# Scoring rows turned on TensorE, and a difference step that makes its state first

## The reference

```python
r = sigmoid(i_r + h_r); z = sigmoid(i_z + h_z)       # i = x @ W_ih + b_ih, h = state @ W_hh + b_hh
n = tanh(i_n + r * h_n)
state = (1 - z) * n + z * state                      # 1024 steps, one after the other
...
xn = (x - mean) * rsqrt(var + 1e-5) * gamma + beta
input_sigs = sign(xn)                                # 1024 signs per token
tile_sigs[e, features of e] = sign(mean(slopes[e]))  # zero elsewhere
best cluster = argmax over 8 of input_sigs @ cluster_sigs.T
tile_idx     = argmax of input_sigs @ tile_sigs.T within that cluster
u = clip((x_slice - min of the expert) / (max - min + 1e-8)); out = (base + slope * local) * scale
```

## Time and profile before

| | |
|---|---|
| median of three runs | 2458.68 us |
| the profiled execution, its own time | 2458.56 us |
| its span, first to last instruction | 2457.0 us |
| TensorE busy | 2338.7 us, 95% |
| VectorE, ScalarE, GpSimd busy | 1298.6, 658.6 and 215.8 us |
| difference stage | 2151.3 to 2358.4 us, 207.1 us |
| tail | 2358.4 to 2457.0 us, 98.6 us |

### The profile page before, as it was taken

The page is one execution under the profiler, slowest core; times in us unless marked ns, Lnnn a source line. Parts: engine busy times, 40 slices in busy tenths (PEclk is TensorE's granted clock), DMA queues, the critical chain, the costliest instruction groups (busy, mean ns, idle before and its releaser), DMA issues.

```text
span 2457.0 us, 83441 instructions
## 1 busy us (share of the span) xinstructions
PE 2338.7 (95%) x35188; PEld 1285.9 (52%) x35188; DVE 1298.6 (53%) x2691; ACT 658.6 (27%) x1333; POOL 215.8 (9%) x440
## 2 busy tenths in 40 slices
PE   7999999999999999999999999999999999977736
PEld 3444444444444445555666666666666666643412
DVE  4322121212122357676666655666666667788877
ACT  3200000000001133333333332333333333355530
POOL 0000000000000000000000000111111111123225
PEclk9999999999999999999999999999999999999965
DMA  7693131313143455454444444444444444478830
GB/s 238 206 338 126 51 129 52 129 52 128 48 145 103 154 166 157 139 158 123 136 133 132 132 142 103 117 118 120 113 119 116 115 120 121 117 228 232 234 89 5
DMA packets 177346, 330.78 MB, mean 135 GB/s; under 512 B 24272, under 2 KB 87168, under 8 KB 176192
## 3 DMA queue, kind: packets, MB, share of 16 engines
q1 hardware_dynamic: 145360, 267.53, 34.8%
q0 software_dynamic: 7680, 17.57, 4.9%
q10 hardware_dynamic: 24192, 44.05, 4.8%
HBM read 222.39 MB, written 156.77 MB: 154 GB/s over the span
## 4 chain that ended last, share of the span: by engine, by line
PE 51%; DVE 5%; DMA 3%; issue 2%; POOL 1%; ACT 0%; DVEq 0%; SPq 0%; POOLq 0%; ACTq 0%
PE banks L605 45%; PE banks L653 2%; DMA hs_scratch<-h 2%; PE banks L654 2%; PE banks L655 2%; DMA x_keep<-hs_scratch 1%; POOL y L1581 1%; DVE banks L1562 0%; DVE n_sum L912 0%; DVE sums L917 0%; PE banks L1487 0%; DVE z_old L902 0%; DVE rn L882 0%; POOL late_out L1189 0%; DVE x_keep L946 0%
## 5 line engine op out<-in xcount | busy, mean ns | idle before, releaser
L605 PE MATMUL banks<-w_hi,hi 128*32 128x512 f16 (+1 forms) x13712 | 604.6, 331 | 17.4 <-DVE hi L922 11.2
L605 PEld LDWEIGHTS banks<-w_hi,hi 128*32 128x32 f16 x13712 | 362.0, 98 | 240.0 <-issue 31.6
L325 DVE SCALAR_TENSOR_TENSOR out_stage<-acc,bias_row 128x512 f32<-128x512 f32 x168 | 115.9, 690 | 611.0 <-PE acc L386 611.0
L605 PE MATMUL banks<-w_lo,hi 128*32 128x512 f16 (+1 forms) x8192 | 355.0, 326 | 0.0
L605 PE MATMUL banks<-w_hi,lo 128*32 128x512 f16 (+1 forms) x8192 | 355.0, 326 | 0.0
L384 PE MATMUL acc<-w_hi,x_even 128*128 128x512 f16 x768 | 292.3, 381 | 12.7 <-DVE x_even L317 11.1
L385 PE MATMUL acc<-w_hi,x_even 128*128 128x512 f16 x768 | 292.2, 380 | 0.0
L386 PE MATMUL acc<-w_lo,x_even 128*128 128x512 f16 x768 | 292.1, 380 | 0.0
L605 PEld LDWEIGHTS banks<-w_lo,hi 128*32 128x32 f16 x8192 | 219.1, 97 | 113.7
L605 PEld LDWEIGHTS banks<-w_hi,lo 128*32 128x32 f16 x8192 | 219.1, 97 | 113.7
L739 ACT ACTIVATE rz<-sums 128x512 f32<-128x512 f32 x176 | 110.9, 630 | 530.2 <-DVE sums L887 530.2
(11 more groups left out here) (172 smaller groups left out, 2250.2 us busy)
## 6 DMA issues: line engine op xcount, KB each, us to landing
stage<-gi_scratch SPq DMA_DIRECT2D x704, 96.0 KB
gi_scratch<-out_stage ACTq DMA_DIRECT2D x168, 256.0 KB, 2.0
stage<-sums_scratch SPq DMA_DIRECT2D x40, 512.0 KB
stage<-in_xT SPq DMA_DIRECT2D x32, 512.0 KB, 6.4
y<-in_x_rows SPq DMA_DIRECT2D x32, 512.0 KB, 4.5
hs_scratch<-h SPq DMA_DIRECT2D x128, 128.0 KB
x_keep<-hs_scratch SPq DMA_DIRECT2D x32, 512.0 KB, 3.9
y<-hs_scratch POOLq DMA_DIRECT2D x32, 512.0 KB, 8.1
```

The lines of the kernel that those rows point to most:

```text
L325: nc.vector.scalar_tensor_tensor(out=out_stage[:, tb], in0=acc[e % BANKS][:], scalar=UNSCALE, in1=bias_row[:].rearrange("p q f -> p (q f)" ...
L605: last = nc.tensor.matmul(bank[q * COLS:(q + 1) * COLS, 0:b - a], state[:, s, j], w[:, j, q * QW + a:q * QW + b], start=first and j == 0, ...
```

## The change

In the difference stage and the tail of the first pass, gamma, beta and the sign leave VectorE. TensorE turns xhat in eight 128x128 pieces, two groups of four (pe_rows), into PSUM. There a feature is a partition, so gamma and beta are the scale and bias of ScalarE's Sign, eight activations of 128x128 (act_half_signs). TensorE then multiplies the signs by score_w, 128x8 per piece, whose entries are the experts' signs (pe_scores). VectorE picks from the scores in PSUM (dve_route with by_product). The normalisation of a tile moves from the end of its loop round into the first set-step of the next, the route from the middle of a round to its end, the turning of the one-hot one tile later; so one tile more is left for the tail.

In a difference set-step VectorE now makes h = new_n + z_old first and then diff = 256·h − warm-up state; old_less is gone.

SyncE: the load of the sums (in full steps the inputs) is issued once n_sum has been read, ahead of the store of h, no longer behind it; h_tok of a tile is loaded in the first set-step of the next round; the copies of x into y for tiles 21 to 31 are issued in rounds 1 to 11, so that none is left in the difference stage. Once, near 1145 us, gamma, beta and the signs are loaded as columns (feature_cols, 3 x 1024 single elements). GpSimd builds score_w at the start (one memset, two affine_selects) and multiplies it once by the signs.

```diff
+        def pe_rows(pe, T, g):
+            if g == 0:
+                pe.wait_ge(xhat_ready, T)
+                pe.sem_inc(wait_carrier, 1)
+            pe.wait_ge(half_signs, nth(T) * 2 + (g - 1))
+            pe.sem_inc(wait_carrier, 1)
+            for k in range(KB // 2):
+                last = nc.tensor.transpose(row_bank[g][:, k * P:(k + 1) * P], xhat[:, (g * (KB // 2) + k) * P:(g * (KB // 2) + k + 1) * P],
+                                           t["ident"][:])
+            last.then_inc(rows_turned, 1)
+        def pe_scores(pe, T):
+            pe.wait_ge(half_signs, nth(T) * 2 + 2)
+            pe.sem_inc(wait_carrier, 1)
+            for k in range(KB):
+                last = nc.tensor.matmul(score_bank[:, k * BLOCK_SLICES:(k + 1) * BLOCK_SLICES], signs_t[:, k], score_w[:, k],
+                                        start=True, stop=True)
+            last.then_inc(scores_ready, 1)
...
+                    tile(DIFF_TILE - 1, turn=False)
+                    pe.wait_ge(rows_split, 6)
+                    pe.sem_inc(wait_carrier, 1)
+                    pe.wait_ge(ends_step, 4)
+                    pe.sem_inc(wait_carrier, 1)
                     with pe.Fori(DIFF_TILE, TILES) as i:
-                        pe_run(pe, pair_of(0, i), 0, seeds, DIFFS)
-                        pe_run(pe, pair_of(0, i), 1, seeds, DIFFS, after=(None, lambda: pe_turn(pe, i - 1)))
+                        def turn_and_rows():
+                            pe_turn(pe, i - 2)
+                            pe_rows(pe, i - 1, 0)
+                        pe_run(pe, pair_of(0, i), 0, seeds, DIFFS, after=(None, turn_and_rows))
+                        pe_run(pe, pair_of(0, i), 1, seeds, DIFFS, after=(lambda: pe_rows(pe, i - 1, 1), lambda: pe_scores(pe, i - 1)))
...
+                if first:
+                    pe_turn(pe, T - 2)
+                    scores(T - 1)
...
+                if first:
+                    pe.wait_ge(pass_judged, 1)
+                    scores(T)
...
+        def act_half_signs(act, T, g):
+            if g == 0:
+                act.wait_ge(tile_id_ready, T - 1)
+                act.sem_inc(wait_carrier, 1)
+            act.wait_ge(rows_turned, nth(T) * 2 + (g - 1))
+            act.sem_inc(wait_carrier, 1)
+            for k in range(KB // 2):
+                at = g * (KB // 2) + k
+                last = nc.scalar.activation(signs_t[:, at], row_bank[g][:, k * P:(k + 1) * P], ACT.Sign,
+                                            bias=feature_cols[:, 1, at:at + 1], scale=feature_cols[:, 0, at:at + 1])
+            last.then_inc(half_signs, 1)
...
+                        def signs_and_sum():
+                            act_half_signs(act, T - 1, 1)
+                            act_sum(act, T, signed)
+                        act_step(act, it, 0, 0, turns, DIFFS, gates(0, 0), lambda: act_normalise(act, T - 1, i - 2))
+                        act_step(act, it, 0, 1, turns, DIFFS, gates(0, 1), lambda: act_half_signs(act, T - 1, 0))
+                        act_step(act, it, 1, 0, turns, DIFFS, gates(1, 0, lambda: act_hit(act, T - 2, i - 3)), signs_and_sum)
+                        act_step(act, it, 1, 1, turns, DIFFS, gates(1, 1), lambda: act_squares(act, T, signed))
...
+                if first:
+                    act_normalise(act, T - 1, TILES - 2)
+                    act_hit(act, T - 2, TILES - 3)
+                signs_of(T - 1)
...
-            if mode in (DIFFS, LAST):
-                dve.wait_ge(z_old_ready[s], n)
-                dve.wait_ge(warm_state_loaded[s][u], from_diffs(it) * 8 + 16 * (1 + u))
-                nc.vector.scalar_tensor_tensor(out=old_less[:, s], in0=z_old[:, s], scalar=S_SCALE, in1=warm_state[:, s, u],
-                                               op0=ALU.mult, op1=ALU.subtract).then_inc(old_less_ready[s], 1)
             dve.wait_ge(not_z_ready[s], n)
             dve.wait_ge(n_ready[s], n)
             nc.vector.tensor_tensor(new_n[:, s], not_z[:, s], n_act[:, s], ALU.mult).then_inc(new_n_ready[s], 1)
             dve.wait_ge(z_old_ready[s], n)
             dve.wait_ge(new_n_ready[s], n)
-            if mode in (DIFFS, LAST):
-                dve.wait_ge(old_less_ready[s], from_diffs(it) + (u + 2))
-                nc.vector.scalar_tensor_tensor(out=diff[s], in0=new_n[:, s], scalar=S_SCALE, in1=old_less[:, s],
-                                               op0=ALU.mult, op1=ALU.add).then_inc(diff_made[s], 1)
-                dve.wait_ge(diff_made[s], from_diffs(it) + (u + 2))
-                if mode == DIFFS:
-                    dve.wait_ge(diff_seen[s], from_diffs(it) + (u + 1))
-                nc.vector.transpose(flat(hi[:, s]), diff[s]).then_inc(hi_ready[s], 1)
             if mode not in (HEADS, KEPT):
                 dve.wait_ge(h_stored[s][u], it * 16 + (16 - pair_of(0, 0) * 16))
             if mode == KEPT:
                 dve.wait_ge(state_out_ready[s], it * 2 + (u + 1 - WARM_HEADS))
             nc.vector.tensor_tensor(h_new, new_n[:, s], z_old[:, s], ALU.add).then_inc(h_ready[s], 1)
+            dve.wait_ge(h_ready[s], n)
             if mode in (DIFFS, LAST):
+                dve.wait_ge(warm_state_loaded[s][u], from_diffs(it) * 8 + 16 * (1 + u))
+                nc.vector.scalar_tensor_tensor(out=diff[s], in0=h_new, scalar=S_SCALE, in1=warm_state[:, s, u],
+                                               op0=ALU.mult, op1=ALU.subtract).then_inc(diff_made[s], 1)
+                dve.wait_ge(diff_made[s], from_diffs(it) + (u + 2))
+                if mode == DIFFS:
+                    dve.wait_ge(diff_seen[s], from_diffs(it) + (u + 1))
+                nc.vector.transpose(flat(hi[:, s]), diff[s]).then_inc(hi_ready[s], 1)
                 return
...
+            if by_product:
+                dve.wait_ge(scores_ready, nth(T))
+                done[0] += 1
+                dve.sem_inc(route_step, 1)
+            else:
+                dve.wait_ge(signs_ready, T)
+                step(nc.vector.tensor_reduce(scores[:], signs[:].rearrange("p (t j) -> p t j", j=SLICE), AX.X, ALU.add), done)
...
+                    if modes[0] == DIFFS:
+                        dve_route(dve, T - 1, True)
+                    elif modes[1] == FULL:
+                        dve_signed(dve, T)
...
+                    with pool.Fori(DIFF_TILE, TILES) as i:
+                        pool_keep(pool, i - 2, i - 3)
+                        pool_add(pool, i, i - 1, True)
+                        pool_pick(pool, i - 2, i - 3)
+                        pool_scale(pool, i, i - 1)
...
+            for f, src in enumerate((gamma.rearrange("o (k p) -> p (o k)", p=P), beta.rearrange("o (k p) -> p (o k)", p=P),
+                                     sign_dram.rearrange("t j -> (t j)").rearrange("(k p) -> p k", p=P))):
+                sp.dma_start(feature_cols[:, f], src, allow_slow_non_contiguous=True).then_inc(curves_loaded, 16)
...
-                def steps(i, after):
+                def steps(i, before=None, after=None):
                     for u in range(2):
                         for s in range(SETS):
+                            if before:
+                                sp.wait_ge(n_sum_ready[s], steps_to(pair_of(p, i), u))
+                                sp.sem_inc(wait_carrier, 1)
+                                before(s, u)
+                            if (u, s) == (0, 0) and not (isinstance(i, int) and i == 0):
+                                load_h_tok(sp, p * TILES + i, i - 1)
                             store_h(sp, pair_of(p, i), i, s, u)
-                            after(s, u)
-                    load_h_tok(sp, p * TILES + i + 1, i)
+                            if after:
+                                after(s, u)
...
+                def next_state(i):
+                    def load(s, u):
                         sp.wait_ge(hi_ready[s], steps_to(pair_of(0, i), u) + 2)
                         sp.sem_inc(wait_carrier, 1)
                         load_state(sp, i * 2 + (2 + u), s, u)
                     return load
-                def rows(i, load):
+                def rows(i, late=False, then=None):
                     def after(s, u):
-                        load(s, u)
-                        if s == 0 and u == 1:
+                        if then:
+                            then(s, u)
+                        elif s == 0 and u == 1:
                             begin_y(sp, i)
+                        if late and s == 1 and u == 1:
+                            begin_y(sp, i + (Y_LATE - 1), late_y_begun)
...
+                    with sp.Fori(2, TILES - Y_LATE + 1) as i:
+                        steps(i, next_gi(i), rows(i, True))
+                with sp.Fori(TILES - Y_LATE + 1 if first else 2, DIFF_TILE - 1 if first else TILES - 1) as i:
+                    steps(i, next_gi(i), rows(i))
                 if first:
                     with sp.Fori(DIFF_TILE - 1, TILES - 1) as i:
-                        steps(i, rows(i, next_diffs(i)))
```

(10 more changed lines are left out.)

144 lines of the change are left out of this document (89 added, 55 removed).

## The result

| | before | after |
|---|---|---|
| median | 2459.26 us (4 runs) | 2432.27 us (4 runs, 2431.53 to 2437.44) |
| profiled execution | 2458.56 us | 2431.53 us |
| its span | 2457.0 us | 2430.0 us |
| difference stage | 207.1 us | 181.4 us |
| tail | 98.6 us | 99.0 us |

The ratio after to before is 0.9893, 95% interval 0.9877 to 0.9910: 27.0 us between the medians. Two terms of the sum missed: a round of the stage takes 18.2 us and not 17.2, and the tail gained nothing.

What follows compares the result with a forecast made beforehand. VectorE bounds the difference stage before, TensorE after, at 16.1 + 1.1 = 17.2 us a round. The sum: 2458.6 - 32 (stage) + 1.1 (start) - 0.6 (tail) + 0 (columns) = 2427 us; 8-in-10 range 2409 to 2446.

Steps and rivals of the forecast that it cites:

- VectorE: Difference round: set-step 3.25 us with seven instructions, route 1.40, VectorE's round 14.4 us against 17.9 before.
- TensorE's own round: Difference round: four set-steps 13.9, transposes 1.8, products 0.3, turn 0.1; 16.1 us, making TensorE the bound.
- The allowance: Difference round: 1.1 us added to TensorE's 16.1, from nothing to the old 2.5, giving 17.2 us.
- Rival 1: Difference stage: h_tok's load waits for the addition into y; round 18.0 to 19.0 us, 2440 at 18.5; chance 0.22.
- signs of being wrong: Difference stage: no VectorE gap, TensorE waiting for xhat or Signs each round, h_tok waiting for the addition, or TensorE standing near 1150 us.
- the forecast's own band: Whole kernel: a difference round of 16.5 to 18.0 us, times 2420 to 2435 us; chance 0.58.
- The transfers' side: Difference stage: copy into y leaves, an eighth of the bytes; about 14 us of DMA work remain per round of some 17.
- The low clock: Difference stage: low-clock share should go, granted clock above 0.95; opposing rival, gaps at 1.2 GHz, 2491 us, chance 0.08.
- Ends: Start and tail: GpSimd's three added instructions +1.1 us, tail -0.6 us; ends of -4 and +4 kept for the tail.
- The feature columns: Load of 3072 single elements near 1150 us: 4 or 18 us of all 16 engines, cost 0 to 6, taken as 0.

Runs made afterwards that it cites:

- the fastest version: Kernel after with the fourth h's store before the sums load, h_tok's sum behind the gates, addition into y issued late and not waited for: 2419.32 us.
- the sum behind the gates: Kernel after with ScalarE's sum over h_tok moved from ahead of the fourth set-step's rz to behind its gates, ahead of its tanh: 2432.60 us.

## Why the prediction came out as it did

**VectorE: right.** From the fourth rn (2236.44) to the route behind its set-step (2239.68) are 3.24 us with seven instructions (forecast 3.25), hi ends 3.29 behind rn (3.33), the route takes 1.46 us (1.40). VectorE, the bound before, is busy for 129.44 of 181.4 us.

**TensorE's own round: right as a sum, 16.1 us, by parts that cancel.** The round of 2156.70 to 2172.82 has it, and so has the fastest version. But the first group of four transposes takes 0.54 to 0.58 us until the next instruction and the second 0.49, about 1.05 us for the 1.8 of the sum, where the lower bound (0.9) was nearer; the eight scores take 0.49 for 0.3. With the turn that is 13.9 + 0.58 + 0.49 + 0.49 + 0.17 = 15.6. The other half microsecond is a wait for xhat (0.54 to 0.71 us in the fastest version), which the prediction had said would not be. In the kernel after this wait is 1.36 us in eight of the ten rounds, and a wait for xhat in each round was one of the prediction's own signs of being wrong. That the sum gave 16.1 is luck.

**The allowance: the step that failed, in size.** I took 1.1 us a round for transfers and ScalarE's order, "from nothing to the old 2.5"; it is 18.2 - 16.1 = 2.1, and 2.6 beyond TensorE's own 15.6. (The old 2.5 had the long round in it; without that the kernel before exceeds VectorE's 17.9 by 2.0.) Rival 1 had the place (h_tok, the store of h, a round of 18.0 to 19.0) and the wrong link: the addition's landing is not waited for. I counted 14.3 us around the addition and never added up the loop beside it: store 9.78, h_tok 3.83, sum 1.15, 3.2 us from there to the next store (2254.33 to 2257.52) and 0.5 of hand-overs, 18.5 us. The landing of this store was nowhere in my rows, though the chain of the kernel before had it at 7.1 to 7.5 us; in the kernel after it stands right behind 512 KB of sums and takes 8.5 to 9.8. The prediction booked the earlier load of the sums as a gain only. The remark that ScalarE's work behind the third tanh was "inside the allowance" was not far off for its work (the four Signs take 1.49 us for 1.05 forecast) but left out its wait for h_tok, 16.0 us in the stage.

The Trainium skill has a rule that bears on this landing ("DMA: Bandwidth & Descriptors", Queues, rings and completion order): a transfer's count is written to its semaphore only once all earlier writes of the same DMA engine have been done, over all its queues. By that rule a store is late by whatever writes stand ahead of it, also those of another engine's queue. The runs agree in direction: 8.5 to 9.8 us behind the load of the sums, 8.2 to 8.5 ahead of it, 9.9 to 11.8 with the copies back. None of them counted the writes.

The time was met better than the round. A round of 18.2 us lies in rival 1's band (18.0 to 19.0), the 2432 us lie in the forecast's (2420 to 2435): the first two rounds were short (16.1 and 17.2 us), and the stage began 1.7 us earlier for no reason that the runs show. So that the forecast's own band was hit is in part luck.

**The transfers' side had a gain that I priced at nothing.** The moved copies are worth 12 to 14 of the 27 us, the largest part that was isolated. The difference step is worth nothing in the old order and 4.1 us in the new one. What is left is the 13.0 us between the kernel before and the one with the copies back. In it are the turning on TensorE, the new difference step, the sums issued earlier and the long round of the kernel before, 4.8 us, which the other does not have (its largest gap between gathers is 0.84 us); these were not separated.

**The low clock: gone, as forecast.** The stage runs at 1.00, with TensorE's waits at 1.4 us or less. On the rule of the Trainium skill ("TensorE: Matmul & The Clock Gate", PE-mode transpose), that a transpose does not count as work for the clock: no run bears it out as a cost here. Neither eight transposes a round (1.00) nor sixteen (1.00 and 0.99) brought the clock down. It was lower, 0.91 to 0.96, in the kernels in which TensorE waited longer.

**Ends.** The first product comes at 11.93 us for 11.09, +0.84 (forecast +1.1). GpSimd's three added instructions lie between 2.45 and 3.32 us.

The tail is 0.4 us longer (forecast -0.6). Its timeline, against the earlier trace rows:

```profile
2345.32 1.24 ACT L835 ACTIVATE x_keep<-x_keep,shift,rstd 128x1024 f32<-128x1024 f32 x1 [3.09 <-POOL shift L1266]
...
2348.02 2.90 ACT L851 ACTIVATE bias_row<-banks,feature_cols 128x128 bf16<-128x128 f32 x8 [1.30 <-PE banks L689]
```

From xhat to the route are 2351.55 - 2346.56 = 5.0 us; 5.8 before, 4.3 forecast. Transposes and Signs follow each other there with nothing beside them, and the eight Signs take 2.90 us for 2.1 forecast. The feature columns cost SyncE 2.0 us of issuing and TensorE nothing to be seen, as taken.

In sum: the stage -25.7 for -32, its earlier start -1.7 (the 0.84 in it), the tail +0.4 for -0.6: 2457.0 - 25.7 - 1.7 + 0.4 = 2430.0 us of span.

## What to carry over

Before a change that makes the bounding engine faster, add up each loop that closes over a round through memory, transfers at their landing times, and not only the engines: here store, load, sum and gate made 18.5 us, where TensorE's first round took 16.1. Read the chain of the kernel before for such a loop: its two transfers were already there. A wait at the head of an in-order queue is paid by everything behind it, so a loop can have a twin through the queue; shorten the link that both share. What is issued just ahead of a small store moves its landing. And before taking a mean over rounds as the price of one, look whether one of them stands out.

## What the runs showed of the hardware

The same store of 128 KB from the same tile landed in 9.9 to 11.8 us with the copies in the stage, in 8.5 to 9.8 behind a load of 512 KB, in 8.2 to 8.5 ahead of it, and within 4.9 to 6.5 where the addition of 512 KB too came behind it. h_tok's load of 512 KB took 3.9 us in the kernel after (median of ten) and 7.0 in the fastest version, where the addition was issued ahead of it.

TensorE stayed at the upper clock through waits of up to 1.4 us in the kernel after, and through one of 1.89 us in that with the sum behind the gates (64 products in 2.79 us behind it). After waits of 1.62 and 1.99 us in one set-step they took 4.37 us. In the kernel with h_tok's load and the sum both later, TensorE waited 1.99 to 2.72 us at the same place in nine rounds: in five the products behind took 4.07 to 4.47 us, in four 2.78, and the length of the wait does not tell which.
